# Turning the heads' sums with VectorE's 32x32 block transposes in place of TensorE's transposes

## The reference

```
x = x + attn(layernorm(x))         # q, k, v normed per head, softmax(q k^T / sqrt(8)) v, then Wo
x = x + ffn(layernorm(x))          # (silu(x wg) * (x wu)) wd, int weights times 1/127
attn: out = einsum('bhqk,bkhd->bqhd', probs, v).reshape(b, s, 128);  return out @ Wo + bo
```

## Time and profile before

| | us |
|---|---|
| median of 3 runs | 344.26 (343.06 to 344.77) |
| profiled execution, own time | 344.02 |
| its span | 342.3 |
| turn 0, first exponential to the next turn's S(0) | 26.49 to 67.67 |
| a turn in the middle, 177.43 to 213.60 | 36.17 |
| turn 7 and tail | 285.72 to 342.3 |

### The profile page before, as it was taken

How to read it: one execution, slowest core, us unless ns; L and a number is a source line. 1 busy time by engine, 2 the same in 40 slices (tenths; PEclk the granted TensorE clock), 3 DMA queues, 4 the chain that set the end, 5 groups by cost and what they waited for, 6 DMA issues and landing times.

```text
span 342.3 us, 10586 instructions
## 1 busy us (share of the span) xinstructions
PE 312.3 (91%) x4116; PEld 144.8 (42%) x4116; DVE 232.5 (68%) x648; ACT 274.1 (80%) x312; POOL 52.5 (15%) x98
## 2 busy tenths in 40 slices
PE   7977858799998999999999999999998998889997
PEld 7963213144234433543354425442442233223576
DVE  5991596868885797768776887688846573433355
ACT  3326967998988899889988998989889997999511
POOL 7701050041002300050004100410021010200020
PEclk9996998999999999999999999999999999999999
DMA  5353112321215113231404130311221123000000
GB/s 156 109 156 124 32 34 79 114 90 63 66 60 156 35 58 101 63 92 61 123 14 139 61 106 17 124 61 53 70 95 61 33 94 114 13 2 3 33 1 31
DMA packets 21717, 24.77 MB, mean 72 GB/s; under 512 B 2096, under 2 KB 17712, under 8 KB 21680
## 3 DMA queue, kind: packets, MB, share of 16 engines
q1 hardware_dynamic: 20544, 23.06, 21.6%
q10 hardware_dynamic: 1136, 1.21, 1.1%
HBM read 15.36 MB, written 8.65 MB: 70 GB/s over the span
## 4 chain that ended last, share of the span: by engine, by line
PE 57%; ACT 20%; issue 12%; DVE 7%; ACTq 2%; DMA 1%; POOL 0%; POOLq 0%; DVEq 0%
PE oacc L928 24%; ACT probs L772 18%; PE side L855 17%; PE scores L913 8%; PE side L848 4%; PE scores L809 1%; PE scores L1021 1%; ACT osb L736 1%; DMA parts_dram<-parts 1%; DVE qk_c L1107 1%; ACTq L423 1%; ACT th L731 1%; DVE v_c L1107 1%; PE side L1021 1%; DVE ht L1164 0%
## 5 line engine op out<-in xcount | busy, mean ns | idle before, releaser
L772 ACT ACTIVATE probs<-scores 128x1536 f32<-128x1536 f32 (+1 forms) x256 | 248.4, 1025 | 38.0 <-PE scores L913 28.9
L928 PE MATMUL oacc<-probs,vaug 128*32 128x512 f32 x1024 | 138.3, 612 | 6.2 <-ACT osb L736 2.7
L913 PE MATMUL scores<-qst,kst 32*128 32x512 f16 x512 | 51.2, 389 | 13.8 <-ACT probs L772 10.7
L582 POOL TENSOR_SCALAR ve<-mv 128x4 f32<-128x4 f32 (+1 forms) x17 | 4.0, 235 | 230.4 <-DVE v_c L1107 136.2
L913 PEld LDWEIGHTS scores<-qst,kst 32*128 32x128 f16 x512 | 13.1, 91 | 57.2 <-ACT probs L772 44.6
L928 PEld LDWEIGHTS oacc<-probs,vaug 128*32 128x32 f32 x1024 | 20.4, 108 | 39.3 <-ACT probs L772 27.8
L855 PE MATMUL side<-x2T_parts,gu_parts 128*32 128x512 f16 x504 | 33.6, 379 | 0.7 <-DVE x2T_parts L1307 0.4
L1107 DVE SCALAR_TENSOR_TENSOR qk_c<-side,rs,wqkv 128x128 f32<-128x128 f32 x64 | 17.9, 344 | 15.2 <-PE side L855 14.9
L855 PEld LDWEIGHTS side<-wqkv,xT 128*32 128x32 f32 x736 | 21.5, 113 | 15.0 <-issue 13.4
L855 PEld LDWEIGHTS side<-x2T_parts,gu_parts 128*32 128x32 f16 x504 | 14.1, 96 | 29.6 <-issue 18.9
L855 PE MATMUL side<-wqkv,xT 128*32 128x128 f32 x736 | 25.2, 279 | 1.0 <-issue 1.0
(11 more groups left out here) (171 smaller groups left out, 320.1 us busy)
## 6 DMA issues: line engine op xcount, KB each, us to landing
parts_dram<-parts SPq DMA_DIRECT2D x15, 256.0 KB, 2.5
qst<-parts_dram SPq DMA_DIRECT2D x15, 256.0 KB, 2.7
kst<-parts_dram SPq DMA_DIRECT2D x15, 256.0 KB, 3.0
x_in<-in_x SPq DMA_DIRECT2D x8, 256.0 KB, 3.3
x_res<-in_x SPq DMA_DIRECT2D x8, 256.0 KB, 3.5
parts_dram<-parts SPq DMA_DIRECT2D x15, 128.0 KB, 1.9
xT<-in_xT SPq DMA_DIRECT2D x7, 256.0 KB, 3.4
out_dram<-y SPq DMA_DIRECT2D x7, 256.0 KB, 2.1
```

Source lines behind the costliest of these rows:

```text
L772: act.activation(out, src, ACT.Exp).then_inc(exp_done, 1)
L913: last = pe.matmul(scores[:, j if j < TRIPLE else TRIPLE + u % 2, :], kst[r, g, kt * P:(kt + 1) * P], qst[r, g, :], start=True, stop=True)
L928: last = pe.matmul(oacc[STRIP * j:STRIP * (j + 1), :], vaug[:, kt, NG * g + j, :], probs[:, kt, j, :], start=first, stop=last_of_half)
```

## The change

The read-out of `oacc` no longer goes over PE. DVE's `transpose` turns each 32x32 block by itself: out of `oacc` straight into `sums_t` (`take_sums`), where strip j's partition q and block b hold query 32b + q of head strip j. `divide` works there into `on_t`, and a second DVE transpose (`turn_heads`) gives `onT` with the heads in another order on the partitions: row 32j + 16o + 8k + d. Wo's rows are brought into that order on the way in. The pieces OT0, OT1 and onT go, as do `copy_o`, `copy_o0` and `copy_onT`. The tables give the side pieces new units and banks, DVE's order is rewritten, and the third tanh moves from unit 11 to 12.

```diff
-SIDE = {0: ["a_v"], 1: ["b_OT1"], 2: ["a_rq", "b_onT"], 3: ["b_Wo"], 4: ["a_rk"], 5: ["e_q"], 6: ["e_k"], 7: ["b_x2T"],
+SIDE = {0: ["a_v"], 1: ["a_rq"], 3: ["a_rk"], 4: ["b_Wo"], 5: ["e_q"], 6: ["e_k"], 7: ["b_x2T"],
-FIRST_SIDE = {1: ["f_q"], 2: ["f_k"], 4: ["a_v"], 8: ["a_rq"], 9: ["a_rk"], 10: ["e_q"], 11: ["e_k"], 12: ["c_OT0"]}
+FIRST_SIDE = {1: ["f_q"], 2: ["f_k"], 4: ["a_v"], 7: ["a_rq"], 8: ["a_rk"], 10: ["e_q"], 11: ["e_k"]}
...
-            TANH_AT = {8: 0, 10: 1, 11: 2}
+            TANH_AT = {8: 0, 10: 1, 12: 2}
...
                 if first:
-                    at_least(pe, osb_done, NO * i + g // 2)
+                    at_least(pe, sums_taken, NO * i + g // 2)
...
-            def copy_o0(b):
-                dve.wait_ge(pv_done, NU * b + NU // NO)
-                at_least(dve, OT_filled, NO * b)
-                dve.tensor_copy(osb[:, :], oacc[:, :]).then_inc(osb_done, 1)
-
-            def copy_onT(b):
-                dve.wait_ge(onT_filled, b + 1)
-                dve.tensor_copy(onT[:, :], side[:, BANK["b_onT"], :])\
+            def take_sums(b, o, half=None):
+                blocks, cols = (slice(0, NB), slice(0, S)) if half is None else (half_blocks[half], half_cols[half])
+                dve.wait_ge(pv_done, NU * b + NU // NO * (o + 1))
+                at_least(dve, on_done, NO * b + o + (half or 0))
+                dve.transpose(sums_t[:, blocks, :], oacc[:, cols].rearrange("p (b q) -> p b q", q=STRIP))\
+                   .then_inc(sums_taken, 1)
+
+            def divide(b, o, half=None):
...
+                dve.reciprocal(rinv[:, blocks, :], sums[:, :, :, HD]).then_inc(rinv_done, 1)
...
+            def turn_heads(b, half=None):
...
+                dve.transpose(onT[:, cols].rearrange("p (b q) -> p b q", q=STRIP), on_t[:, blocks, :])\
                    .then_inc(onT_done, 1)
...
                     first_part(1)
+                    second_part(1)
+                    take_sums(0, 0)
                     centred(2, 0)
-                    second_part(1)
...
-        "Wo": a["L0_attn_Wo"],
+        "Wo": a["L0_attn_Wo"].reshape(NO, PAIR, NG, HD, D).transpose(2, 0, 1, 3, 4).reshape(D, D),
```

More of the change, by code:

```diff
@@ L384, in build @@
                     "rq": (qkf_done, 2, 0), "rk": (qkf_done, 2, 1),
[L385 to L386 removed]
+                    "Wo": (x2_done, 1, 0), "x2T": (x2T_done, 1, 0), "d0": (y_done, 1, 0)}
         read_out.update({f"g{j}": (ga_done, NF, j) for j in range(NF)})
@@ L994, in _ @@
             times_v(B, -1)
-            keep_warm(WARM_LAST["osb"], scores[:, 0, 0:P])
+            keep_warm(WARM_LAST["on"], scores[:, 1, 0:P])
             pe.wait_ge(y_done, B - 1)
[L998 to L1004, removed]
             for half, tiles in enumerate(half_tiles):
@@ L1262, in fill_v @@
                 last.then_inc(vaugA_done if half == 0 else vaugB_done, 1)
[L1264 to L1280, removed]
@@ L1407, in turn @@
                     return
-                if early:
-                    ln1_stats(i + 2)
                 fill_v(i, 1)
+                if behind:
+                    take_sums(i - 1, 1)
                 if ahead:
@@ L1418, in turn @@
                 if behind:
-                    ln2_stats(i - 1)
+                    turn_heads(i - 1)
                 if ahead:
                     affined(i + 1, 1)
-                    first_part(i + 1)
+                if behind:
+                    ln2_stats(i - 1)
                 if early:
@@ L1428, in turn @@
                     centred(i + 2, 1)
-                    later_square(i + 2, 0)
                 if behind:
                     copy_x2T(i - 1)
+                take_sums(i, 0)
+                if early:
+                    later_square(i + 2, 0)
                 if ahead:
-                    copy_o0(i)
+                    first_part(i + 1)
+                divide(i, 0)
+                if ahead:
+                    sums_v(i + 1)
+                if behind:
+                    silu(i - 1, 0, side[:, BANK["b_g0"], :])
                 if early:
                     later_square(i + 2, 1)
+                if behind:
+                    times_up(i - 1, 0, side[:, BANK["b_u0"], :])
                 if ahead:
@@ L1443, in turn @@
                 if behind:
[L1444 to L1447, removed]
                     silu(i - 1, 2, side[:, BANK["b_g2"], :])
-                    times_up(i - 1, 1, side[:, BANK["b_u1"], :])
-                divide(i, 0)
+                    times_up(i - 1, 2, side[:, BANK["b_u2"], :])
                 if ahead:
@@ L1472, in _ @@
             turn(B - 1, "last")
-            lastO = NO * (B - 1)
-            dve.wait_ge(on_done, lastO + 1)
             for half in range(2):
[L1477 to L1486, removed]
-                        out=on[:, ts, h0 * HD:(h0 + NG) * HD].rearrange("p t (j d) -> p t j d", d=HD),
-                        in0=o[:, :, :, HC * k:HC * k + HD],
-                        in1=rinv[:, k, ts, :].unsqueeze(3).broadcast_to((P, HALF_TILES, NG, HD)), op=ALU.mult)
-                last.then_inc(on_done, 1)
-            for half, cols in enumerate(half_cols):
-                dve.wait_ge(onT_filled, B + half)
-                dve.tensor_copy(onT[:, cols], onTs[half][:, 0:S // 2]).then_inc(onT_done, 1)
+                take_sums(B - 1, 1, half)
+                divide(B - 1, 1, half)
+                turn_heads(B - 1, half)
             dve.wait_ge(xbo_done, B)
```

76 lines of the change are left out of this document (33 added, 43 removed).

## The result

The changed kernel takes 345.0 us (median of 16 runs, 343.13 to 346.26) against 343.97 us before (16 runs, 342.73 to 344.77). The ratio is 1.0035, 95% interval 1.0021 to 1.0050: 0.35% slower, within the half per cent that the prediction called "same", and 0.8 us under the forecast of 345.8. The profiled execution took 345.28 us, its span is 343.6 (342.3 before).

What follows compares the result with a forecast made beforehand. PE and ACT bound the kernel in turns. Turn 0 +6.6, middle turns -2.75, near turn -0.6, last turn -1.2, tail -0.55 sum to +1.5 us: 345.5 profiled, forecast 345.8; own range 344 to 348, wider range 342.4 to 350.0.

Steps and rivals of the forecast that it cites:

- The bound: Whole kernel: PE and ACT set the pace in turns; removing a transpose piece leaves a unit at 2.0 us.
- Rival 1: All turns: TensorE is the bound, pieces give back 1.9 us a turn, 337; chance 0.13 together with rival 5.
- The transpose's price: DVE: a transpose out of oacc takes 0.70 us; DVE gets some 0.3 to 0.7 us more per turn.
- rival 2: DVE: four-byte transposes run at half pace, 1.22 us each, giving 353; chance 0.12.
- Middle turn: Five middle turns: 0.55 us won each in the first half, 0 to 0.1 counted in the second; -2.75 in all.
- Near, last, tail: Near turn -0.6 us, last turn -1.2 from both read-outs, tail -0.55 between V(15) and x2.
- Turn 0: First turn: one unit lost by rq's place, late sums idle PE 3.3 us, lower clock follows; +6.6, bounds +4.7 and +7.5.
- Rival 3: Turn 0: the second stall does not lower the clock, -1.9 us, 343.9; chance 0.15.
- rival 5: Turn 0: the stall is absent, only the lost 2.2 us unit remains, 341.5; chance 0.13 together with rival 1.
- rival 4: Turn 0 worse than counted, or middle turns win only half as late silu holds g1: 347.5 to 349.5; chance 0.20.
- The sum: Whole kernel: all terms together +1.5 us, profiled execution 345.5 for 344.02, forecast 345.8; chance 0.40.

Runs made afterwards that it cites:

- the piece in unit 2: Changed kernel with four PE transposes of 128x128 (0.66 us, identity into a free bank) added in unit 2 of turns 1 to 7: 346.1 us, 1.0042.
- warm stall: Changed kernel with 13 matmuls of 128 columns by the identity on PE in turn 0's unit 9 stall: 342.56 us, 0.9949.
- sums early: Changed kernel with one line moved: in turn 0 DVE takes unit 7's sums right behind reading rq, ahead of rk and both parts: 339.97 us, 0.9884.
- rq and rk in their old units: Changed kernel with turn 0's sums taken ahead of rq's reading, and rq and rk back in units 8 and 9: 338.31 us, 0.9824.
- ACT's copy: Changed kernel with an idle 128x512 copy on ACT behind the exponentials of unit 0 in turns 1 to 7: 345.77 us, 1.0044.

## Why the prediction was right, point by point

- **The bound.** PE and ACT in turns, unit by unit, was the right reading. Rival 1 (PE the bound, 1.9 us a turn) is excluded by the piece in unit 2: 0.66 us of PE for at most 0.05 us of time.
- **The transpose's price.** 0.70 us was taken, 0.713 and 0.702 were measured, so rival 2 (1.22) did not come. The Trainium skill (Vector Engine (DVE) Microarchitecture Reference, section 3.8) has one element per cycle per lane for the transposing front-end. The trace agrees in so far as a transpose keeps the pace of the copy of the same shape, which took 0.692. I undersized the small operations: reciprocal and product took 0.345 and 0.470, not 0.226 and 0.285, and their busy time is 12.3 us where the two of each had 12.8 (5.5 and 7.3). DVE's busy time rose by 5.6 us in all, 0.7 per turn, the top of my 0.3 to 0.7.
- **Middle turn.** 0.55 was predicted and 0.82 measured: 0.69 in the first seven units and 0.13 in the rest. This term was too small by a third. V(0) came at 0.44 behind S(1), 0.1 earlier than I reckoned, unit 2 took 1.95 for my 2.0, and the second half, which I had put at 0 to 0.1, gave 0.13. Several things moved there at once (OT0, g2, the third tanh), and no run takes them apart. The room at g1 shrank from 1.13 to 0.23 us, 0.9 for my 1.0.
- **Near, last, tail.** Turn 6, from S(0) to S(0), gave 0.67 (35.37 for 36.04; predicted 0.6), turn 7 0.74 (predicted 1.2), the tail 1.04 (predicted 0.55). Of the tail, 0.65 lies in the stretch that I had priced.
- **Turn 0.** +6.6 was predicted, +7.4 measured. The term that was too small is the lower clock: V(8) began at 57.65 for my 57.5, but from there to S(11) it took 5.9 us for my 5.1. At full clock it is 3.2, as counted (warm stall). All three parts are shown by themselves: the late read-out with the clock behind it is 4.5 net and 5.3 in its own units (sums early), of which the clock is about 2.3 (warm stall), rq's place is 2.3, and the order of the parts the last 0.6. The 0.6 is a part that I missed: I wrote that from S(11) on the units run as before. They did in the changed kernel, 3.33 for 3.32, since there everything waited for the stall; the cost only comes out once the stall is gone. So the parts do not add up as independent terms, but undoing all three gives back the 24.25 us of before (24.26). Rival 3 (the clock stays up) is excluded by the granted 0.50 from 57.4 to 62.0, rival 5 by the 3.39 us wait. Of rival 4, the dearer turn 0 came, by 0.8 us; the middle turns won more than I had put and not half.
- **The sum.** Turn 0 came out 0.8 dearer and the rest 1.2 better than the forecast's 5.1 (-6.3 in the table, in which 0.2 is the smaller idle at the loop's entry, 0.78 for 1.00). That the total of the profiled execution came within 0.2 us of the forecast's (345.28 for 345.5) is in part luck, as these two errors offset each other. The mechanism on either side was right. The prediction gives two ranges, 344 to 348 and 342.4 to 350.0; the measured time lies in both.

The change was thus worth 6 us, and three lines of order in the first turn spent them. With these lines undone the kernel is 1.9% faster than before the change (0.9812), and with PE kept busy in the first stall 2.3% (0.9772).

## What to carry to other kernels

Price what an edit takes out unit by unit: the same 0.66 us of TensorE work cost at most 0.05 us in a unit that another engine sets and 0.48 in the one beside it. When a read-out moves from one engine to another, look at each place where it is issued, the start-up above all: an in-order engine with other work queued ahead takes sums late that have long been ready (3.45 us late here). And a stall of TensorE can cost more than its length: behind the 3.4 us of idling here the clock was granted at 0.50, and that cost about 2.3 us more.

## What the runs showed of the hardware beyond that

The granted clock fell without any long stall just ahead. With the sums taken early, PE's last idle gaps ahead of the fall were 1.06 and 0.80 us, and yet S(13) at 62.98 took 0.61 and V(12) 1.94 us. The window over it (of the kernel with the sums taken early; columns as above):

```profile
62.90:66.50 3.60, 3.52 (x24) 0.62 (x24) 3.29 (x10) 2.84 (x5) 0.00 (x0) 0.55 0.00 0
```

In the changed kernel and in the one before it the same units ran at full clock. So they did in the kernel with rq and rk in their old units, where PE idled 1.64 us ahead of S(12). What decides it was not tried.

PE's first pass of its loop over the turns holds an idle gap that no wait explains. It is 1.00 us in the kernel before, 0.78 in the changed one, and 1.51 and 1.60 in two kernels that differ from these only by a few matmuls. These matmuls are not the whole cause: four kernels with the changed kernel's PE program, line for line, have 0.78, 0.80 (ACT's copy), 1.03 (sums early) and 1.12 (each transpose out of `oacc` twice). These two rows are from the changed kernel and from the one with four transposes in unit 2:

```profile
113.97 0.42 PE L839 MATMUL side<-wqkv,xT 128*32 128x128 f32 x6 [0.78 <-issue]
```

```profile
115.17 0.62 PE L839 MATMUL side<-wqkv,xT 128*32 128x128 f32 x10 [1.51 <-issue]
```

Differences of under a microsecond between kernels with different code are therefore better read from the turns than from the total.
